# A graph layer: skip projection fused with the node projection, and two tables of sums in place of four

## What is computed

```python
h = maximum(layernorm(x), 0)
s, v = h[:, :64], h[:, 64:].reshape(N, 32, 3)
skip_s, skip_v = s @ W_skip0, einsum('nmi,mk->nki', v, W_skip1)      # 96 and 32x3 numbers a node
s, v = s @ W_nl0, einsum('nmi,mk->nki', v, W_nl1)                    # 64 and 32x3 numbers a node
w = relu(edge_feature @ W_fc1) @ W_fc2                               # 224 weights an edge
xs, xv = s[dst], v[dst]                                              # gather
tp = products of w, xs, xv and the edge's direction                  # 96 scalars, 128 vectors
agg = segment_sum(tp, src, N) / 32                                   # scatter-add
out_s = agg_s @ W_out_s + skip_s
out_v = agg_v @ W_out_v + skip_v
out = x + concat(silu(out_s[:, :64]), sigmoid(out_s[:, 64:]) * out_v)
```

## Time and profile before

| | |
|---|---|
| median of 3 runs | 1441.69 us (1435.4 to 1458.28) |
| profiled execution | 1451.14 us, of which the span of instructions is 1449.3 us |
| busy in the span | PE 1171.7, DVE 894.6, ACT 448.1, POOL 1107.3 us |
| mean granted clock of TensorE | 0.763 |
| DMA | 144.09 MB, 99 GB/s over the span |
| DMAs by POOL | 416 gathers, 416 scatters |

### The profile page before, as it was taken

The page is one execution under the profiler, slowest core; times in us unless marked ns, Lnnn a source line. Parts: engine busy times, 40 slices in busy tenths (PEclk is TensorE's granted clock), DMA queues, the critical chain, the costliest instruction groups (busy, mean ns, idle before and its releaser), DMA issues.

```text
span 1449.3 us, 23307 instructions
## 1 busy us (share of the span) xinstructions
PE 1171.7 (81%) x5766; PEld 958.0 (66%) x5766; DVE 894.6 (62%) x3688; ACT 448.1 (31%) x868; POOL 1107.3 (76%) x853
## 2 busy tenths in 40 slices
PE   8799898898878987898878888798987988888700
PEld 5577777676766766677666667676766767666600
DVE  8348756666565666656566665666656566665519
ACT  5134323333223333333323332333332333323300
POOL 1538888888888888888888888888888888888874
PEclk9579967778688877868787887877777776778755
DMA  6544554554545555454554545455454554545574
GB/s 249 168 164 90 89 96 83 91 88 78 101 79 94 86 83 95 77 101 79 94 87 77 100 78 97 82 90 89 78 100 78 93 86 79 98 78 86 53 205 156
DMA packets 118198, 144.09 MB, mean 99 GB/s; under 512 B 30880, under 2 KB 91552, under 8 KB 118176
## 3 DMA queue, kind: packets, MB, share of 16 engines
q0 software_dynamic: 79872, 75.03, 36.5%
q1 hardware_dynamic: 36576, 61.34, 13.9%
q10 hardware_dynamic: 1728, 7.47, 1.3%
HBM read 88.56 MB, written 55.21 MB: 99 GB/s over the span
## 4 chain that ended last, share of the span: by engine, by line
DMA 45%; POOL 26%; issue 18%; PE 6%; DVE 3%; POOLq 1%; ACT 0%; SPq 0%; DVEq 0%
DMA sums<-to_add,add_idx 44%; POOL rows L302 19%; POOL sums L320 7%; PE w_ps L428 1%; PE d_ps L399 1%; PE d_ps L397 1%; PE o_ps L399 1%; PE o_ps L397 1%; PE t_ps L443 0%; POOLq L287 0%; PE o_ps L461 0%; DMA h_sb<-sums 0%; PE o_ps L380 0%; PE o_ps L378 0%; PE w_ps L380 0%
## 5 line engine op out<-in xcount | busy, mean ns | idle before, releaser
L320 POOL DMA_INDIRECT sums<-to_add,add_idx x416 | 664.8, 1598 | 126.8 <-issue 78.0
L302 POOL DMA_INDIRECT rows<-node_table,to_idx x416 | 410.3, 986 | 181.1 <-issue 102.1
L729 DVE TENSOR_TENSOR products_space<-rows,rhat 128x256 f32<-128x256 f32 (+2 forms) x520 | 170.5, 393 | 454.4 <-DMA rows<-node_table,to_idx 453.6
L461 PEld LDWEIGHTS o_ps<-w,pT 128*128 128x128 f32 (+1 forms) x2496 | 403.4, 246 | 40.2 <-issue 32.3
L461 PE MATMUL o_ps<-w,pT 128*128 128x96 f32 (+1 forms) x2496 | 420.8, 334 | 2.7 <-ACT pT L577 2.7
L443 PE MATMUL t_ps<-w,products_space 128*128 128x128 f32 (+1 forms) x1248 | 238.5, 325 | 128.9 <-DVE products_space L758 128.8
L443 PEld LDWEIGHTS t_ps<-w,products_space 128*128 128x128 f32 (+1 forms) x1248 | 181.9, 171 | 152.8 <-issue 119.6
L428 PE MATMUL w_ps<-w,hid 64*128 64x224 f32 x832 | 275.4, 463 | 2.6 <-ACT hid L569 2.6
L476 PE MATMUL d_ps<-msg,same 128*128 128x192 f32 x832 | 225.3, 403 | 50.2 <-ACT to_add L597 30.5
L586 ACT ACTIVATE msg<-o_ps 128x448 f32<-128x448 f32 x208 | 113.1, 544 | 449.4 <-PE o_ps L461 263.1
L476 PEld LDWEIGHTS d_ps<-msg,same 128*128 128x128 f32 x832 | 165.6, 231 | 128.8 <-issue 127.2
(11 more groups left out here) (115 smaller groups left out, 516.7 us busy)
## 6 DMA issues: line engine op xcount, KB each, us to landing
from_row<-nodes_row SPq DMA_DIRECT2D x52, 512.0 KB
ef<-edge_t SPq DMA_DIRECT2D x52, 256.0 KB
rows<-node_table,to_idx POOLq DMA_INDIRECT x416
sums<-to_add,add_idx POOLq DMA_INDIRECT x416
sums<-zeros ACTq DMA_DIRECT2D x8, 672.0 KB
sums<-zeros SPq DMA_DIRECT2D x4, 672.0 KB
x_sb<-x SPq DMA_DIRECT2D x5, 400.0 KB, 6.8
node_table<-node_rows SPq DMA_DIRECT2D x5, 400.0 KB, 2.4
```

The lines of the kernel that those rows point to most:

```text
L302: pool.indirect_dma_start(rows[:, u, j, SC:CR], None, table, bass.IndirectOffsetOnAxis(ap=to_idx[:, par, h * J + j:h * J + j + 1], axis=0) ...
L320: pool.indirect_dma_start(sums[j], bass.IndirectOffsetOnAxis(ap=add_idx[:, u, j:j + 1], axis=0), to_add[:, u, j, :], None, compute_op=ALU.add,
L461: ins = nc.tensor.matmul(o_ps[m][:, base + oc:base + oc + n], pT[c][u % 2][:, cols], w[0:ROWS[c], wc:wc + n], start=(q == 0 and c == 0), s ...
L729: ins = nc.vector.tensor_tensor(vecs(crs[:, dst, :, i0 * V:(i0 + n) * V], n), vecs(rows[:, u, :, VE + v0 * V:VE + (v0 + n) * V], n), unit( ...
```

## The change

The skip projection is fused with the node projection: `project_node` moves 160 columns (skip scalars and node scalars) and 192 (node vectors and skip vectors), and ACT copies all 352 into `node_out`. From there SP writes the middle 160 to `node_table` and the outer 96 and 96 to table `sums_0`, which thus starts with the skip rows in place of zeros. `skip_products`, `copy_skip` and POOL's adds in the last stage are gone.

There are two tables of sums. Tile j of a group goes to table j % 2, so two scatters of one group go to the same table. Scatters 0 and 1 wait for scatters 2 and 3 of the group before; scatters 2 and 3 wait for scatters 0 and 1 of their own group. The order of four gathers and then four scatters in a step stays. Only `sums_1` and the spare rows of `sums_0` are zeroed, by five DMAs on SP's queue; ACT issues none. The last stage loads two tables and adds them once on DVE.

```diff
-    sums = [nc.dram_tensor(f"sums_{j}", [TABLE_ROWS, M], F32, kind="Internal").ap() for j in range(J)]
+    sums = [nc.dram_tensor(f"sums_{j}", [TABLE_ROWS, M], F32, kind="Internal").ap() for j in range(TABLES)]
...
             sp.wait_ge(zero_set, 1)
-            for part_of_sums in ZERO_PARTS[:EARLY_ZEROS]:
-                set_zero(sp, *part_of_sums)
+            for a, e in ZERO_RUNS:
+                sp.dma_start(sums[1].rearrange("(p t) m -> p t m", p=P)[:, a:e, :],
+                             zeros[:, 0:e - a, :]).then_inc(zeroed, 16)
+            sp.dma_start(sums[0][NPAD:TABLE_ROWS, :], zeros[:, 0, :]).then_inc(zeroed, 16)
...
             for c in range(STEPS):
                 sp.wait_ge(rows_ready, (c + 1) * CH)
-                sp.dma_start(table_d[:, step_of(c), :], node_rows[:, step_of(c), :]).then_inc(table_out, 16)
+                sp.dma_start(table_d[:, step_of(c), :], node_out[:, step_of(c), SO:SO + F]).then_inc(table_out, 16)
+                sp.dma_start(sums_d[0][:, step_of(c), 0:SO], node_out[:, step_of(c), 0:SO]).then_inc(skip_out, 16)
+                sp.dma_start(sums_d[0][:, step_of(c), SO:M], node_out[:, step_of(c), SO + F:]).then_inc(skip_out, 16)
...
-                if valid(g - 1, GROUPS):
-                    pool.wait_ge(added[j], 16 * g)
+                if j >= TABLES:
+                    pool.wait_ge(added[j - TABLES], 16 * (g + 1))
+                    tick()
+                elif valid(g - 1, GROUPS):
+                    pool.wait_ge(added[j + TABLES], 16 * g)
                     tick()
                 else:
-                    pool.wait_ge(zeroed, 16 * len(ZERO_PARTS))
+                    pool.wait_ge(zeroed, 16 * (len(ZERO_RUNS) + 1))
+                    pool.wait_ge(skip_out, 16 * 2 * STEPS)
                 pool.indirect_dma_start(
-                    sums[j], bass.IndirectOffsetOnAxis(ap=add_idx[:, u, j:j + 1], axis=0),
+                    sums[j % TABLES], bass.IndirectOffsetOnAxis(ap=add_idx[:, u, j:j + 1], axis=0),
                     to_add[:, u, j, :], None, compute_op=ALU.add,
                 ).then_inc(added[j], 16)
...
-            pool.wait_ge(skip_ready, SKIP_PAIRS)
-            for c, tt in enumerate(LAST):
-                pc = part[c][:, :, 0:tt.stop - tt.start]
-                pool.wait_ge(three_in[c], 16 * 3)
-                nc.gpsimd.tensor_tensor(pc[:, 2], pc[:, 2], skip[:, tt, :], ALU.add).then_inc(with_skip, 1)
...
-                nc.tensor.matmul(op[:, 0:S], hT[0:S, t, 0, :], w[0:S, W_NS + SO:W_NS + SO + S],
+                nc.tensor.matmul(op[:, 0:SO + S], hT[0:S, t, 0, :], w[0:S, W_NS:W_NS + SO + S],
                                  start=True, stop=False, skip_group_check=True)
-                nc.tensor.matmul(op[:, S:F], hT[0:3 * V, t, 1, :], w[0:3 * V, W_NV:W_NV + 3 * V],
+                nc.tensor.matmul(op[:, SO + S:SO + S + 6 * V], hT[0:3 * V, t, 1, :], w[0:3 * V, W_NV:W_NV + 6 * V],
                                  start=False, stop=True, skip_group_check=True).then_inc(projected, 1)
...
-                nc.scalar.activation(node_rows[:, t, :], (o_ps + w_ps)[t % 4][:, 0:F], ACT.Copy,
+                nc.scalar.activation(node_out[:, t, :], (o_ps + w_ps)[t % 4][:, 0:SO + S + 6 * V], ACT.Copy,
                                      scale=node_std[:, 1, t:t + 1]).then_inc(rows_ready, 1)
...
             def total(c, tt):
                 pc = part[c][:, :, 0:tt.stop - tt.start]
-                dve.wait_ge(three_in[c], 16 * 3)
-                nc.vector.tensor_tensor(pc[:, 0], pc[:, 0], pc[:, 1], ALU.add).then_inc(pair_sum, 1)
...
-                nc.vector.tensor_tensor(pc[:, 0], pc[:, 0], pc[:, 2], ALU.add).then_inc(total_ready, 1)
+                dve.wait_ge(tables_in[c], 16 * TABLES)
+                nc.vector.tensor_tensor(pc[:, 0], pc[:, 0], pc[:, 1], ALU.add).then_inc(total_ready, 1)
```

More of the change, by code:

```diff
@@ L66 @@
 LAST = [slice(a, min(a + n, NT)) for a, n in ((0, 5), (5, 5), (10, 5), (15, 5), (20, 3), (23, 2))]
[L67 removed]
+TABLES = 2
 ZR = 7
 ZERO_RUNS = [(a, min(a + ZR, TABLE_ROWS // P)) for a in range(0, TABLE_ROWS // P, ZR)]
[L70 to L71 removed]
 EARLY_GROUPS = 2
@@ L163, in build_program @@
         added = [sem(f"added{j}") for j in range(J)]
[L164 to L168, removed]
+        tables_in = [sem(f"tables_in{c}") for c in range(len(LAST))]
+        total_ready, gate_ready, gated, out_ready, stored = (
+            sem(n) for n in ("total_ready", "gate_ready", "gated", "out_ready", "stored"))
         x_d = x.rearrange("(p t) f -> p t f", t=NT)
@@ L173, in build_program @@
         sums_d = [s[0:NPAD, :].rearrange("(p t) m -> p t m", t=NT) for s in sums]
[L175 to L181, removed]
+        spent = node_out[:, :, :].rearrange("p t f -> p (t f)")
+        spent_h = h_sb[:, :, :].rearrange("p t f -> p (t f)")
+        size = TABLES * CH * M
+        part = [flat[:, k * size:(k + 1) * size].rearrange("p (j t m) -> p j t m", j=TABLES, t=CH)
+                for flat, k in ((spent, 0), (spent, 1), (spent, 2), (spent, 3), (spent_h, 0), (spent_h, 1))]
         gates = to_add[:, :, :, :].rearrange("p u j m -> p (u j m)")[:, 0:NT * SO].rearrange("p (t s) -> p t s", s=SO)
@@ L494, in step @@
                 merge(g - 3, u3, 1)
-                if isinstance(g, int) and g == 0:
-                    for n in range(SKIP_PAIRS):
-                        skip_products(n)
             fc1(0, 0, 0)
@@ L546, in _ @@
                     copy_products(t - 1)
-            def copy_skip(n):
-                act.wait_ge(skip_done, n + 1)
-                for q, t in enumerate(range(2 * n, min(2 * n + 2, NT))):
-                    ins = nc.scalar.activation(skip[:, t, :], (d_ps, o_ps[0])[n % 2][:, q * M:(q + 1) * M], ACT.Copy,
-                                               scale=node_std[:, 1, t:t + 1])
-                ins.then_inc(skip_ready, 1)
-            later_zeros = ZERO_PARTS[EARLY_ZEROS:]
-            def next_zeros(i):
-                if isinstance(i, int) and later_zeros:
-                    set_zero(act, *later_zeros.pop(0))
             def hidden(b, par):
@@ L615, in step @@
                 collect(g - 3, u3, 1)
-                if isinstance(g, int) and g == 0:
-                    for n in range(SKIP_PAIRS):
-                        copy_skip(n)
-                        if n % 4 == 0:
-                            next_zeros(1)
             hidden(0, 0)
```

66 lines of the change are left out of this document (13 added, 53 removed).

## The result

| | before | after |
|---|---|---|
| median of the runs timed together | 1438.55 us (4 runs, 1435.23 to 1458.28) | 1501.08 us (4 runs, 1498.84 to 1509.48) |
| ratio after / before | | 1.0453, interval 1.0393 to 1.0514 |
| profiled execution | 1451.1 us, span 1449.3 | 1498.84 us, span 1497.0 |
| start to first scatter | 110.0 us | 87.4 us |
| first to last scatter | 1285.0 us | 1380.7 us |

The kernel became slower by 4.5%; the forecast was 1485 us. The lower three rows of the table are read from the profiled executions; they add up to 47.7 us more, of which the loop takes 95.7 and from which start and end give back 22.6 and 25.4.

The account below looks back on a forecast made before the run. POOL's in-order queue of gathers and scatters was taken as the bound from first to last scatter. Start, end and loop summed as 1449.3 - 24.7 - 24 + 92 = 1492.6 us, scaled to a median of 1485, range 1427 to 1515.

Parts of the forecast that it names:

- (a): POOL's loop: scatters 2 and 3 wait for landings of their own group; 0.88 us x 104 groups = 92 us more, bounds 0 and 125.
- 0.58 a group for scatter 2: POOL's loop: scatter 2 starts 4.37 us after scatter 0 (landing 3.58 plus start 0.79) in place of 3.79.
- 0.3 a group for long landings: POOL's loop: landings of 3.6 to 5.16 us beside the `ef` load cost 0.3 us a group, an estimate, bounds 0 and 0.6.
- The start of 0.79 us: POOL: a DMA instruction whose wait ends late pays some 0.79 us to get going, which the queue hides otherwise.
- (b): Start, up to the first scatter: without the skip products it comes at 85.3 us, 24.7 earlier; gain of 16 to 28 us.
- I allow 1 us over 25 tiles, bounds 0 and 5: Projection at the start: ACT's wider copy is hidden by its idle unless PE gets slower too; 1 us allowed for that.
- the filling of the pipeline: Start: from first gather to first scatter, 20.4 + 24.4 = 44.8 us once the skip products are gone.
- (c): Last stage: shorter last landing, no POOL adds, one add a chunk in place of two; 24 us less, bounds 18 and 28.
- the last step: Whole time: profiled ratio 1494.4 / 1451.1 = 1.030 times the median of 1441.7 gives 1485 us.
- Nobody waits: First rival, POOL's loop: landing plus start stays under 3.79 us, so scatter 2 gets through; 1393 us, chance 0.08.
- the hidden start: Second rival, POOL's loop: the 0.79 start is partly hidden, only long landings cost, 0.35 us a group; 1429 us, chance 0.17.
- Start not given back, longer landings: Third rival: start gives 16 in place of 25 us, landings cost 0.6 us a group on top; 1525 us, chance 0.1.

Follow-up runs that it names:

- four tables: The changed kernel with four tables in place of two and the old waits, a group's distance, skip projection still fused: median 1420.4 us, ratio 0.981 to the kernel before.
- two and two: The changed kernel with POOL's order as two gathers, scatters 0 and 1, two gathers, scatters 2 and 3: median 1465.7 us, ratio 1.012 to the kernel before.

## Why the prediction was right

**The bound.** That POOL's queue sets the pace, and that the 44% of "DMA sums<-to_add" in the chain of before were waits that the sequencer took ahead of time, held: with four tables nothing was idle, and only the shorter distance made such a wait felt.

**(a) The loop,** forecast +92 us, measured +95.7. Its parts: 0.58 a group for scatter 2 is 60 us; measured (0.835 - 0.305) x 104 = 55. The 0.3 a group for long landings is 31 us; measured at scatter 3 (0.591 - 0.305) x 104 = 30, with 5 more before scatters 0 and 1, all in the ending. Not foreseen were 6 us of busier instructions. The start of 0.79 us, which decided against both rivals on the fast side, came from two rows of the start-up and was confirmed by the run in which each scatter waits.

**(b) The start,** forecast -24.7, measured -22.6. The step that was mis-sized is the projection's "I allow 1 us over 25 tiles, bounds 0 and 5": it was 5.4, outside its own bounds, since PE sets that pace and its matmuls grew with their columns. I had looked at ACT's idle before its copies, which says who waits for whom, and priced only the one who waits. The table write was 0.4 us late where 1.4 were put, an estimate that had no row behind it, and the filling of the pipeline took 43.5 us where 44.8 were put.

**(c) The end,** forecast -24, measured -25.4. The last landing took 4.40 us in place of the 3.6 put, the load 5.25 for 5.82; the adds cost what was read from the rows of before.

**From the span to the median.** Of the 16 us between 1485 and 1501 the three terms make 4.4 (the span was 1497.0 where the sum gave 1492.6), and the new kernel's median lies 2.2 above its profiled execution. The other 9.4 are the last step: I scaled the sum down by 0.65% because the profiled execution of before lay above its median. That execution's skip products ran at a granted clock of 0.50; the new kernel has no such stage. Profiled against profiled the ratio is 1.033, close to the forecast's 1.030; by the medians it is 1.045. The executions of before that set its median seem to lose less at the start than the profiled one did, so the fusion gives less back. I take this from the levels of the times; no run isolates it. How many executions of before fall on which level is chance with four of them: beside the later runs its median was 1451 to 1455. The measured time lies in the stated range of 1427 to 1515 us, but the working of the forecast's own range, 1455 to 1510, isn't whole: added up and scaled like the forecast, the bounds of (a) to (c) give some 1386 to 1532 us.

**The rivals.** "Nobody waits" and the hidden start fell with the two runs that add only waits. The Trainium skill's 2.0 us plus bytes over 436e3 (page "DMA: Bandwidth & Descriptors", section "Anatomy of one DMA — SWDGE (gpsimd) path"), 2.2 us as an estimate for this size, stays below every landing of an accumulating scatter here: their median is 3.6 us on each page that gives one, and even the shortest by its packets is 3.0, in a run of the kernel before. "Start not given back, longer landings" overshot: 22.6 of 24.7 us came back, and the long landings cost what was put.

## What to carry to other kernels

Before reducing the number of buffers that a chain of writes rotates through, compare two figures from the timeline: the natural distance of two writes to the same buffer, and landing plus the start behind a felt wait (3.6 + 0.75 us here); below it each turn pays, from some 0.7 us above it (5.1 us) the wait for a usual landing is free, and long landings beside bulk loads need their own allowance. A chain of waits full of landings doesn't tell which side one is on, since the sequencer may have taken them ahead of time; idle before the instruction does. And when a stage grows, price the engine that is waited for, not the one that waits.

## What the runs showed of the hardware

- A start of some 0.75 us stands between a wait that ends late and an indirect DMA of POOL: 4.42 to 4.58 us from scatter to scatter in the run where each waits, with a landing of 3.6; over its 319 felt waits never less than 0.755. It is absent when the instruction was queued in time (0.305 us between any two).
- An indirect DMA on POOL is mostly cheaper behind its own kind: gathers 1.03, 0.99, 0.95, 0.95 us, scatters 1.62, 1.58, 1.56, 1.55 us (medians by place in four tables). Ordering them in pairs in place of fours cost 30 us over 832.
- A load of 512 KB issued within a microsecond behind a scatter lengthened its landing from 3.2 to 4.3 us (by packets), one of 256 KB from 3.3 to 3.8; with the features cut short in the second case it was 3.3 everywhere.
- PE's matmuls before the first gather took 0.90 and 1.01 us in the profiled executions of two fused kernels (two and two, four tables) and 0.54 and 0.59 in the others, for the whole projection. The granted clock in the windows view was 1.00 from 0 to 42 us in both cases, so there the durations tell it and the column doesn't: the two slow traces hold no record of the clock before 94 and 97 us, and the view puts 1.00 where it has none.
